# A four-part network on one core: clamps left out, two stage starts reordered, and a batch loop written out

## The chip, the core and the metric

The kernel runs on one core of one Trainium2 chip. The core has a matrix engine (TensorE, PE in the rows, with its weight loads as PEld), VectorE (DVE), ScalarE (ACT), GpSimd (POOL) and SyncE (SP), which in this kernel issues every DMA. Each engine works through its own list of instructions in order and waits on semaphores. The metric is the time of one run on the device in microseconds (us); lower is better.

## The reference, cut to what matters

Batch 8, 512 rows of 256 features, a context of 1024 rows of 192 features, all float32.

```
x = x + xattn0(layernorm(x), ctx)   # 16 heads of 64, softmax over 1024 keys
x = x + experts(layernorm(x))       # router on row 0 picks 2 of 8 experts, gelu MLP 256-256-256, mean
x = x + xattn1(layernorm(x), ctx)   # 16 heads of 16; the keys are the values v
x = x + quantised_mlp(layernorm(x)) # 256-1024-256

# quantised_mlp
W_sim = clip(round(W * s), -128, 127) / s,          s = 127 / max|W| per column or row
x_sim = clip(round(x * t), -32768, 32767) / t,      t = 32767 / max|x|
hidden = gelu(x_sim @ W_in_sim + b_in)
out = quantise_a16(hidden) @ W_out_sim + b_out
```

Since every scale divides by the largest magnitude, the scaled values lie within plus or minus 127 or 32767, up to rounding.

## The kernel before, in words

The four parts run one behind the other, with a barrier of all engines between them. The first attention takes 2006 us of the 3537 us and is not touched.

**Experts** (`experts`). SP loads row 0 of each batch (x8), the first batch's rows, the router's weights, and then the rows of batches 1 to 7 by seven DMAs of 512 KB (line 960). VectorE normalises x8, TensorE computes the router's scores, and VectorE's last routing step (L1083) finds the chosen experts. SP copies the choice to one row by a DMA (line 964), reads an expert's number from it and issues that expert's weights (lines 974 to 980: w1 and w2 of 256 KB, b1, b2), two experts per batch, double-buffered by batch. TensorE (L1016) needs both experts' weights of its batch. VectorE waits for all seven loads before it normalises batch 1.

**Second attention** (`second_attention`). A head prepares batch 0: the projection weights are split in a high and a low float32r part (ScalarE L1579, VectorE L1698), GpSimd fills constant regions (eight memsets, L1727) and then computes the reciprocal deviation (rstd, L1732) for the layer norm; VectorE normalises the rows (L94), TensorE transposes them (L1338) and projects values and queries of head group 0 in three chunks through one PSUM bank, `ps_x` (L1350, L1356), each split by ScalarE (L1539) and VectorE (L1613) before the next may start. Four DMAs spread the queries (qz, L1272), and 32 score blocks are reduced to row maxima (TensorE L1370, VectorE L1619), between which TensorE projects v (L1461). `combine` (L1626) ends the maxima; then the main part starts. It is one body per batch, `batch(b, left)`: four head groups (`attend`: scores, exp on ScalarE L1531, probabilities times v L1397, the next group's maxima), then v of the next batch (L1461) and the output projection with its addition (VectorE L1691). Batches 0 to 5 are one hardware loop per engine (`Fori`), batches 6 and 7 are already written out.

**Last part** (`quantised_layer`). Weights are quantised on VectorE (`quantise_weights`); rows are normalised while they load again; then x is rounded and split, TensorE computes the hidden layer (L2028), ScalarE the gelu (L2043), VectorE each tile's largest value (L1995). The output stage works per batch in four chunks of 1024 columns: VectorE clips and rounds (L2111, L2118), ScalarE subtracts the rounding constant and scales (L2166, L2178), VectorE forms the low part (L2125), TensorE multiplies (L2215, L2217), and VectorE adds the bias and input (`finish`, L2133) for the previous batch behind chunk 1. VectorE rounds three chunks ahead. GpSimd adds the output bias once per batch (L2200). Adding and then subtracting MAGIC (12582912.0) rounds a float32 to an integer.

Of the kernel before, what the change touches and what calls it, by code (L numbers as in the profile page):

```python
# [5 lines left out]
F32 = mybir.dt.float32  # L6
# [882 lines left out]
def experts(nc, x_sb, ident, mhalf, d, x_before):  # L889

    with ExitStack() as ctx:
# [41 lines left out]
        s_x0 = sem("first_x")  # L933
        s_xrest = sem("other_x")
# [18 lines left out]
        def _(sp):  # L953
# [12 lines left out]
            with sp.Fori(0, B // 2) as i:  # L966
                for u in range(2):

                    sp.wait_ge(s_x, QT * (2 * i + u))
                    for k in range(2):  # L970
# [10 lines left out]
                                     ).then_inc(s_w[u], 16)  # L981

# [82 lines left out]
        def _(dve):  # L1065
# [75 lines left out]
def second_attention(nc, x_sb, ident, ident_r, mhalf, d, ctx_parts, x_dram, spare, s_win, s_xs):  # L1141


    with ExitStack() as ctx:
# [55 lines left out]
        s_raw = sem("raw_weights")  # L1200
        s_wh = sem("weights_high")
# [42 lines left out]

        raw_p = prob[:, 0, 0:2, :]
# [11 lines left out]
        def _(sp):  # L1257
            sp.dma_start(raw_p[:, 0], d["v1_wp"][0:P].rearrange("p g n -> p (g n)")).then_inc(s_raw, 16)
            sp.dma_start(raw_p[0:DC1, 1], d["v1_wp"][P:DC].rearrange("p g n -> p (g n)")).then_inc(s_raw, 16)
            sp.dma_start(raw_v[:, 0], d["v1_w"][0:P]).then_inc(s_raw, 16)  # L1260
            sp.dma_start(raw_v[0:DC1, 1], d["v1_w"][P:DC]).then_inc(s_raw, 16)
            sp.dma_start(wqp[:], d["q1_wp"].rearrange("(c k) g n -> k c g n", k=P)).then_inc(s_const, 16)
            for t, a in ((bqp, "q1_b"), (bvp, "v1_bp"), (bv, "v1_b"), (bo, "o1_b")):
                sp.dma_start(t[:], d[a]).then_inc(s_const, 16)
            sp.dma_start(wo[:], d["o1_w"].rearrange("(c p) n -> p c n", p=P)).then_inc(s_const, 16)

# [54 lines left out]
            sp.wait_ge(s_fill, FILLS)  # L1321
# [4 lines left out]
            with sp.Fori(0, B - 2) as b:  # L1326
                batch(b, 2)
# [5 lines left out]
        def _(pe):  # L1333
            def turn_queries(b, c):

                pe.wait_ge(s_ln, 14 * (b + 1))
                for qt in range(QT):
                    mm = pe.transpose(ps_x[:, qt * P:(qt + 1) * P], xn[:, qt, c * P:(c + 1) * P], ident[:])  # L1338
                mm.then_inc(s_tr, 1)

            def project(G, n, c, between=None):


                if c > 0:

                    pe.wait_ge(s_lo, 3 * G + c)
                if c < 2:
                    keys = slice(c * 512, (c + 1) * 512)
                    for step, (context, piece, rows) in enumerate(ctx_weights):
                        mm = pe.matmul(ps_x[:], wvp[0:rows, piece, n, :], context[:, keys],  # L1350
# [4 lines left out]
                else:  # L1355
                    pe.matmul(ps_x[:], wqp[:, 0, n, :], xnT[:, 0, :], start=True, stop=False)  # L1356
                    if between:
                        between(1)
                    pe.matmul(ps_x[:], wqp[:, 1, n, :], xnT[:, 1, :], start=False, stop=True).then_inc(s_kq, 1)
# [140 lines left out]
            pe.wait_ge(s_xnT, DCH)  # L1500
            pe.wait_ge(s_ctx, 48)
            pe.wait_ge(s_const, 16 * NCONST)
# [12 lines left out]

            pe.wait_ge(s_lo, 6)
            max_rows(0, 0)
# [8 lines left out]
        def _(act):  # L1526
# [7 lines left out]
            def split_high(G, n, c):  # L1534
# [789 lines left out]
```

## Time and profile before

| what | value |
|---|---|
| median of 3 runs | 3534.97 us (3531.8 to 3538.29) |
| profiled execution, its own time | 3538.93 us |
| its span | 3537.1 us |
| stretch 0 to 2006.5 us | first attention |
| 2006.5 to 2164.4 us | experts, 157.9 us |
| 2164.4 to 2231.6 us | second attention's head, 67.2 us |
| 2231.6 to 3286.4 us | its eight batches, 1054.8 us |
| 3286.4 to 3340.4 us | last part: weights, normalisation, largest x |
| 3340.4 to 3419.4 us | last part: hidden layer, 79.0 us |
| 3419.4 to 3537.1 us | last part: output stage, 117.7 us |

The span is measured from the first to the last instruction; the execution's own time is 1.8 us longer. Shares of busy time over the whole span hide that each stretch has another engine that is never idle, so the stretches are read one by one.

### The profile page before, as it was taken

What the parts mean: (1) busy time and instruction counts of PE and PEld (TensorE: products, weight loads), DVE (VectorE), ACT (ScalarE), POOL (GpSimd) and SP (SyncE); (2) the same over time, 40 slices, a digit from 0 to 9 for tenths busy, and PEclk for the clock granted to TensorE, in tenths of its full rate; (3) what the DMA queues carried; (4) which work ended last, traced back from release to release, by engine and by line L of the source; (5) the groups of instructions that cost most, each with busy time, mean ns of one, the idle gap of its engine ahead of it and who ended that gap; (6) DMA issues with size and microseconds to landing.
All of it is one profiled execution on the core that took longest, in us unless ns stands there. A gap on an engine that the chain in (4) does not pass through costs nothing. (4 is left out here: it accounts for less than half of the span.)

```text
span 3537.1 us, 49438 instructions
## 1 busy us (share of the span) xinstructions
PE 3266.3 (92%) x14300; PEld 1892.3 (53%) x14300; DVE 2383.8 (67%) x3762; ACT 1675.0 (47%) x1904; POOL 1294.1 (37%) x609
## 2 busy tenths in 40 slices
PE   6999999999999999999999596899999999999576
PEld 4556556555565565565555354455555555554366
DVE  4675675665756756746656243777788778876799
ACT  3443443443434434434434121656556566566376
POOL 1764764756647647746656422000000000000101
PEclk9999999999999999999999897999999999999698
DMA  7564554545544545535355223334334333343202
GB/s 179 118 142 114 119 136 111 129 107 132 131 127 116 132 114 128 138 100 137 98 134 127 81 83 85 86 91 105 88 92 100 93 92 96 97 93 72 67 18 77
DMA packets 265101, 379.07 MB, mean 107 GB/s; under 512 B 35944, under 2 KB 170672, under 8 KB 265008
## 3 DMA queue, kind: packets, MB, share of 16 engines
q1 hardware_dynamic: 265008, 378.06, 43.2%
q8 instruction: 31, 0.51, 0.1%
q14 instruction: 62, 0.51, 0.0%
HBM read 82.22 MB, written 27.26 MB: 31 GB/s over the span
## 5 line engine op out<-in xcount | busy, mean ns | idle before, releaser
L863 POOL TENSOR_TENSOR a_prob_sum<-a_prob_sum,a_prob 128x1024 f32<-128x1024 f32 x384 | 924.2, 2407 | 113.7 <-ACT a_prob L588 88.2
L588 ACT ACTIVATE a_prob<-a_t 128x1024 f32<-128x1024 f32 x512 | 518.2, 1025 | 741.8 <-PE a_t L433 734.5
L1619 DVE TENSOR_REDUCE a_mhalves<-a_m 128x1 f32<-128x512 f32 x1024 | 689.6, 688 | 189.1 <-PE a_m L1370 187.2
L731 DVE TENSOR_REDUCE a_mhalves<-a_m 128x1 f32<-128x512 f32 x1024 | 688.7, 690 | 170.7 <-PE a_m L397 153.0
L1531 ACT ACTIVATE a_prob<-a_t 128x1024 f32<-128x1024 f32 x512 | 498.7, 1023 | 145.5 <-PE a_t L1390 140.6
L1370 PE MATMUL a_m<-a_vh,a_qz 128*128 128x512 f32 x1024 | 463.6, 464 | 36.7 <-DVE a_mhalves L1619 19.9
L440 PE MATMUL a_o<-a_prob,a_v_pair 128*64 128x512 f32 x2048 | 495.4, 605 | 0.0
L397 PE MATMUL a_m<-a_kh_n,a_qz 128*128 128x512 f32 x1024 | 408.1, 429 | 22.0 <-DVE a_mhalves L731 9.8
L863 POOL TENSOR_TENSOR a_prob_sum<-a_prob 128x1024 f32<-128x1024 f32 x64 | 151.6, 2369 | 597.1 <-ACT a_prob L588 597.1
L1370 PEld LDWEIGHTS a_m<-a_vh,a_qz 128*128 128x128 f32 x1024 | 189.9, 189 | 325.1 <-DVE a_mhalves L1619 246.8
L425 PE MATMUL a_t<-a_q_hl,a_k_hh 128*128 128x512 f32 x1024 | 334.6, 408 | 10.5 <-DMA a_k_hh<-a_kh_n 10.1
L1390 PE MATMUL a_t<-a_qs,a_vs 128*128 128x512 f32 x1024 | 323.2, 397 | 3.9 <-ACT a_prob L1531 3.6
L433 PE MATMUL a_t<-a_q_hm,a_k_lm 66*128 66x512 f32 x1024 | 321.7, 395 | 0.0
L397 PEld LDWEIGHTS a_m<-a_kh_n,a_qz 128*128 128x128 f32 x1024 | 182.1, 188 | 238.3 <-DVE a_mhalves L731 103.7
L1732 POOL TENSOR_TENSOR a_rstd<-a_veps,mhalf 128x4 f32<-128x4 f32 x8 | 8.2, 1021 | 820.6 <-DVE a_veps L86 820.4
L1397 PE MATMUL a_o<-a_prob,a_v_all 128*18 128x512 f32 x2048 | 269.7, 598 | 0.4 <-ACT a_prob L1531 0.4
L747 DVE RECIPROCAL a_recip<-a_x 128x128 f32<-128x128 f32 x256 | 232.0, 933 | 51.0 <-PE a_x L455 51.0
L722 DVE TENSOR_TENSOR a_ql_n<-a_x,a_qz 64x512 fp32r<-64x512 f32 x128 | 88.1, 688 | 256.5 <-ACT a_qz L604 254.5
L425 PEld LDWEIGHTS a_t<-a_q_hl,a_k_hh 128*128 128x128 f32 x1024 | 182.8, 188 | 111.4 <-DMA a_q_hl<-a_qz 38.9
L440 PEld LDWEIGHTS a_o<-a_prob,a_v_pair 128*64 128x64 f32 x2048 | 124.3, 136 | 219.6 <-issue 190.6
L1390 PEld LDWEIGHTS a_t<-a_qs,a_vs 128*128 128x128 f32 x1024 | 191.5, 189 | 53.2 <-ACT a_prob L1531 14.4
L433 PEld LDWEIGHTS a_t<-a_q_hm,a_k_lm 66*128 66x128 f32 x1024 | 194.0, 189 | 36.3
(242 smaller groups left out, 4135.0 us busy)
## 6 DMA issues: line engine op xcount, KB each, us to landing
a_k_hh<-a_kh_n SPq DMA_DIRECT2D x256, 256.0 KB, 4.5
a_k_lm<-a_kl_n SPq DMA_DIRECT2D x128, 256.0 KB, 4.9
a_v_pair<-a_v_all SPq DMA_DIRECT2D x64, 512.0 KB, 5.2
a_vs<-a_vh SPq DMA_DIRECT2D x256, 128.0 KB, 2.3
a_wk<-wk_parts SPq DMA_DIRECT2D x64, 256.0 KB, 2.8
a_q_hl<-a_qz SPq DMA_DIRECT2D x128, 128.0 KB, 2.4
a_q_hm<-a_qz SPq DMA_DIRECT2D x128, 128.0 KB, 2.4
a_q_hl<-a_ql_n SPq DMA_DIRECT2D x128, 128.0 KB, 2.4
```

The source lines that it names most:

```text
L397: pe.matmul(ps_m[:, n, :], qz[:, hd, qt * P:(qt + 1) * P], kh_n[:, n * 512:(n + 1) * 512], start=True, stop=True).then_inc(s_mx, 1)
L425: pe.matmul(ps_t[t % 2][:, hd, :], k_hh[:, u, hd, keys], q_hl[:, u, hd, :], start=True, stop=False)
L433: mm = pe.matmul(ps_t[t % 2][:, hd, :], k_lm[0:HD0 + 2, u, hd, keys], q_hm[0:HD0 + 2, u, hd, :], start=False, stop=True)
L440: mm = pe.matmul(ps_o[hd * HD0:(hd + 1) * HD0, :], v_pair[:, pr.set, t, hd * HD0:(hd + 1) * HD0], prob[:, t % RING, hd, :], start=(t == 0) ...
L588: nc.scalar.activation(prob[:, t % RING], ps_t[t % 2][:, :, :], ACT.Exp, scale=SCALE0).then_inc(s_exp, 1)
L731: nc.vector.tensor_reduce(mhalves[:, qt, hd, n:n + 1], ps_m[:, n, :], AX.X, ALU.max).then_inc(s_max, 1)
L863: nc.gpsimd.tensor_tensor(acc, prob[:, (t - 1) % RING] if t == 1 else acc, prob[:, t % RING], ALU.add).then_inc(s_acc, 1)
L1370: pe.matmul(ps_m[:, k, :], qz[:, u, h, qt * P:(qt + 1) * P], vh[:, u, k * 512:(k + 1) * 512], start=True, stop=True).then_inc(s_mx, 1)
L1390: mm = pe.matmul(ps_t[j][:, h, :], vs[:, u, 2 * j + h, keys], qs[:, u, 2 * j + h, :], start=True, stop=True)
L1397: mm = pe.matmul(ps_o[QD * h:QD * h + VW, :], v_all[:, t, GH * n + h, :], prob[:, t % RB, h, :], start=(t == 0), stop=(t == KT - 1))
L1531: nc.scalar.activation(prob[:, t % RB, 2 * j:2 * j + 2, :], ps_t[j][:, :, :], ACT.Exp, scale=SCALE1).then_inc(s_exp, 1)
L1619: nc.vector.tensor_reduce(mhalfs[:, u, qt, h, k:k + 1], ps_m[:, k, :], AX.X, ALU.max).then_inc(s_max, 1)
```

## The change

Five things change.

1. In the last part the clamps are left out: a scaled value is multiplied and MAGIC added in one VectorE instruction, where before one multiplied and took the maximum, and a second took the minimum and added MAGIC. That holds for both weights, for x and for the hidden values.
2. In the experts SP loads batch 1's rows only, then fetches the choice; batch 2's rows go between the weights of batches 0 and 1, the other five batches' rows behind them. VectorE's first three normalisations are written out, each waiting for its own load.
3. In the second attention's head the DMAs, the weight splits, the fills and rstd are reordered by need; the first transposes and projections use three PSUM banks instead of one; v is projected whole ahead of the maxima, and group 1's three projections stand behind maxima 1, 8 and 15.
4. ScalarE fills its eight selector blocks between the splits.
5. Batches 0 to 5 of the second attention are written out on TensorE, ScalarE, VectorE and SP. GpSimd keeps a loop.

SP at the start of the experts, first before (names: `e_w`, `e_b` are the experts' weights and biases, `x_sb` the rows, `e_chosen_row` the choice):

```order
L956 DMA x_sb<-x_first 128x4x256
L957 DMA e_wr<-in_wr 128x2x8
L958 DMA e_br<-in_br 8x8
L960 DMA x_sb<-x_first 128x4x256 x7
L964 DMA e_chosen_row<-e_chosen 1x8x8 [waits e_route_dve]
L966 UNCONDITIONAL_BRANCH [waits e_chosen_row]
L966 ISA
L971 ISA [waits e_x_updated]
L971 TENSOR_LOAD e_chosen_row
L971 ISA x2
L974 ISA
L974 DMA e_w<-in_w 128x2x256
```

Here the fetch of the choice (L964) stands behind all the loads of rows. The same place after:

```order
L958 DMA x_sb<-x_first 128x4x256
L959 DMA e_wr<-in_wr 128x2x8
L960 DMA e_br<-in_br 8x8
L964 DMA x_sb<-x_first 128x4x256
L969 DMA e_chosen_row<-e_chosen 1x8x8 [waits e_route_dve]
L978 TENSOR_LOAD e_chosen_row [waits e_chosen_row]
L978 ISA x2
L981 ISA
L981 DMA e_w<-in_w 128x2x256
L983 DMA e_w<-in_w 128x2x256
L985 ISA
```

The fetch (now L969) stands behind batch 1's rows alone; the rows of batch 2 moved between the weights, the rest behind them.

GpSimd at the start of the second attention, first before (`a_qz` the spread queries, `a_mcol` the maxima's column, `a_qs`, `a_v_all`, `a_wvp`, `a_wv` other constant regions):

```order
L1727 MEMSET a_qs 32x2048
L1727 MEMSET a_qs 32x2048 [waits a1_fills]
L1727 MEMSET a_v_all 128x128x2 [waits a1_fills]
L1727 MEMSET a_v_all 128x128 [waits a1_fills]
L1727 MEMSET a_qz 128x4096 [waits a1_fills]
L1727 MEMSET a_mcol 128x4x96 [waits a1_fills]
L1727 MEMSET a_wvp 64x512 [waits a1_fills]
L1727 MEMSET a_wv 64x256 [waits a1_fills]
L1730 UNCONDITIONAL_BRANCH [waits a1_const,a1_fills]
L1730 ISA
L1732 TENSOR_TENSOR a_rstd<-a_veps,mhalf 128x4 [waits a1_ln_steps]
```

Here rstd (L1732) stands behind all the fills. The same place after:

```order
L1780 MEMSET a_wvp 64x512
L1780 MEMSET a_wv 64x256 [waits a1_fills]
L1772 TENSOR_TENSOR a_rstd<-a_veps,mhalf 128x4 [waits a1_ln_steps,a1_fills]
L1780 MEMSET a_qz 128x4096 [waits a1_rstd]
L1780 MEMSET a_mcol 128x4x96 [waits a1_fills]
L1780 MEMSET a_qs 32x2048 [waits a1_fills] x2
L1780 MEMSET a_v_all 128x128x2 [waits a1_fills]
L1780 MEMSET a_v_all 128x128 [waits a1_fills]
L1787 TENSOR_TENSOR x_sb<-x_sb,a_bo 128x1024 [waits a1_ln_steps,a1_const,a1_fills]
```

rstd stood behind eight memsets and stands behind two; the longest, `a_qz`, now comes directly behind rstd.

VectorE in the output stage, batch 0, first before (`f_hid` hidden values, `f_h_low` their low part):

```order
L2111 TENSOR_SCALAR f_hid<-f_hid,f_amax_h 128x2x512
L2125 SCALAR_TENSOR_TENSOR f_h_low<-f_h_int,f_wout_inv,f_h_high 128x512 [waits f_h_high_ready] x2
L2118 TENSOR_SCALAR f_hid<-f_hid 128x2x512 [waits f_rounding_steps]
L2111 TENSOR_SCALAR f_hid<-f_hid,f_amax_h 128x2x512
L2125 SCALAR_TENSOR_TENSOR f_h_low<-f_h_int,f_wout_inv,f_h_high 128x512 [waits f_h_high_ready] x2
L2118 TENSOR_SCALAR f_hid<-f_hid 128x2x512 [waits f_rounding_steps]
L2111 TENSOR_SCALAR f_hid<-f_hid,f_amax_h 128x2x512
L2125 SCALAR_TENSOR_TENSOR f_h_low<-f_h_int,f_wout_inv,f_h_high 128x512 [waits f_h_high_ready] x2
```

Each chunk has two roundings (L2111, L2118) and the low part (L2125). The same place after:

```order
L2156 TENSOR_SCALAR f_hid<-f_hid,f_amax_h 128x2x512 x4
L2164 SCALAR_TENSOR_TENSOR f_h_low<-f_h_int,f_wout_inv,f_h_high 128x512 [waits f_h_high_ready] x2
L2156 TENSOR_SCALAR f_hid<-f_hid,f_amax_h 128x2x512
L2164 SCALAR_TENSOR_TENSOR f_h_low<-f_h_int,f_wout_inv,f_h_high 128x512 [waits f_h_high_ready] x2
L2156 TENSOR_SCALAR f_hid<-f_hid,f_amax_h 128x2x512
L2164 SCALAR_TENSOR_TENSOR f_h_low<-f_h_int,f_wout_inv,f_h_high 128x512 [waits f_h_high_ready] x2
L2156 TENSOR_SCALAR f_hid<-f_hid,f_amax_h 128x2x512
```

One instruction per chunk (L2118) is gone.

The diff, cut to its core:

```
@@ experts, SP and VectorE
-            for b in range(1, B):
-                sp.dma_start(x_sb[:, b * QT:(b + 1) * QT, :], x_view[:, b * QT:(b + 1) * QT, :]
-                             ).then_inc(s_xrest, 16)
+            load_x(1, 2, s_x1)
             sp.wait_ge(s_rt, 8)
             sp.dma_start(chosen_row[:], chosen[:]).then_inc(s_row, 16)
             sp.wait_ge(s_row, 16)
...
+                    if first and u == 0:
+                        load_x(2, 3, s_x2)
+            load_two(0, True)
+            load_x(3, B, s_xrest)
+            with sp.Fori(1, B // 2) as i:
+                load_two(i, False)
...
-            dve.wait_ge(s_xrest, 16 * (B - 1))
-            with dve.Fori(0, B - 1) as b:
+            for b, landed, count in ((0, s_x1, 1), (1, s_x2, 1), (2, s_xrest, B - 3)):
+                dve.wait_ge(landed, 16 * count)
+                normalise_batch(b + 1)
+                update(b)
+            with dve.Fori(3, B - 1) as b:
@@ second attention, TensorE
+        first_banks = [ps_x[:], ps_m[:, 0, :], ps_m[:, 1, :]]
+        FIRST_PROJECTIONS = (1, 8, 15)
...
             for c in range(DCH):
-                if c:
-                    pe.wait_ge(s_xnT, c)
-                turn_queries(0, c)
...
-            pe.wait_ge(s_wl, 4)
-            pe.wait_ge(s_fill, FILLS)
-            for c in range(3):
-                project(0, 0, c)
+                project(0, 0, c, bank=first_banks[c])
...
             for t in range(KT):
                 project_v(0, t)
-                for c in range(CMB * t // KT, CMB * (t + 1) // KT):
-                    max_scores(0, 0, c)
-                if t in (1, 3, 5):
-                    pe.wait_ge(s_lo, 3 + t // 2)
-                    project(1, 1, t // 2)
+            pe.wait_ge(s_lo, 3)
+            for c in range(CMB):
+                max_scores(0, 0, c)
+                if c in FIRST_PROJECTIONS:
+                    project(1, 1, FIRST_PROJECTIONS.index(c))
...
-            with pe.Fori(0, B - 2) as b:
+            for b in range(B - 2):
                 batch(b, 2)
@@ second attention, ScalarE
-            act.wait_ge(s_raw, 64)
+            act.wait_ge(s_raw, 32)
+            split_weights(tasks[0:2])
             for c in range(DCH):
-                keep_turned(0, c)
+                keep_turned(0, c, first_banks[c])
+            split_high(0, 0, 0, first_banks[0])
+            act.wait_ge(s_rawv, 32)
+            split_weights(tasks[2:4])
...
+            for c in range(3):
+                fill_selectors(0, c)
+                split_high(1, 1, c)
@@ last part
             for t in range(FFT):
-                nc.vector.tensor_scalar(w[:, t, :], w[:, t, :], s[:, t:t + 1], -128.0,
-                                        ALU.mult, ALU.max).then_inc(s_wq, 1)
+                nc.vector.tensor_scalar(w[:, t, :], w[:, t, :], s[:, t:t + 1], MAGIC,
+                                        ALU.mult, ALU.add).then_inc(s_wq, 1)
...
-            nc.vector.tensor_scalar(flat, flat, 127.0, MAGIC, ALU.min, ALU.add).then_inc(s_wq, 1)
...
                     def rounded(b):
-                        nc.vector.tensor_scalar(cols, cols, amax["x"][4][:], -32768.0, ALU.mult, ALU.max
-                        nc.vector.tensor_scalar(cols, cols, 32767.0, MAGIC, ALU.min, ALU.add).then_inc(s_xi, 1)
+                        nc.vector.tensor_scalar(cols, cols, amax["x"][4][:], MAGIC, ALU.mult, ALU.add
...
-                def clipped(b, k):
-                    nc.vector.tensor_scalar(cols, cols, amax["h"][4][:], -32768.0, ALU.mult, ALU.max
-                def rounded(b, k):
-                    nc.vector.tensor_scalar(cols, cols, 32767.0, MAGIC, ALU.min, ALU.add).then_inc(s_r, 1)
+                def rounded(b, k):
+                    nc.vector.tensor_scalar(cols, cols, amax["h"][4][:], MAGIC, ALU.mult, ALU.add
```

## Rows read from the trace of the kernel before

**Rows 1.** Busy time by stretch: us, each engine's busy us (instructions), PEclk, DMA.
```profile
2164.40:2231.60 67.20, 37.40 (x112) 22.45 (x113) 35.71 (x75) 17.13 (x23) 13.96 (x10) 0.70 0.38 102
...
3340.40:3419.40 79.00, 63.76 (x259) 49.33 (x259) 68.72 (x112) 60.33 (x75) 0.00 (x0) 0.93 0.00 0
...
3419.40:3537.10 117.70, 78.38 (x512) 74.02 (x512) 112.83 (x160) 75.96 (x96) 22.00 (x8) 0.82 0.22 72
```

**Rows 2.** Timeline, experts' head: start, us, engine, line, operation [idle before <- releaser].
```profile
2011.64 7.28 SPq L960 DMA_DIRECT2D x_sb<-x_first  x7
...
2015.12 0.15 DVE L1083 FIND_INDEX8 e_chosen<-e_top,e_logits 8x8 uint32<-8x8 f32 x1
...
2027.44 0.40 SPq L974 DMA_DIRECT2D e_w<-in_w  x1
...
2035.13 5.31 PE L1016 MATMUL e_h<-e_xnT,e_w 128*128 x8 [13.39 <-DMA e_b<-in_b]
```

**Rows 3.** Timeline, second attention's head.
```profile
2164.53 3.66 POOL L1727 MEMSET a_qs<- 32x2048 f32 x2 [19.21 <-POOLq L891]
...
2166.90 1.31 DVE L86 TENSOR_SCALAR a_veps<-a_mv 128x4 f32<-128x4 f32 x1
...
2169.05 3.52 POOL L1727 MEMSET a_qz<- 128x4096 f32 x1
...
2174.23 1.03 POOL L1732 TENSOR_TENSOR a_rstd<-a_veps,mhalf 128x4 f32<-128x4 f32 x1 [0.24 <-POOL a_wv L1727]
...
2175.29 1.38 DVE L94 TENSOR_SCALAR spare<-x_sb,a_mv,a_rstd 128x256 f32<-128x256 f32 x4 [7.08 <-POOL a_rstd L1732]
...
2181.20 0.79 PE L1350 MATMUL a_x<-a_ctx_high,a_wvp 128*128 128x512 f32 x1 [1.11 <-ACT spare L1545]
...
2193.29 0.69 ACT L1539 ACTIVATE a_qh<-a_x,a_bqp 128x512 fp32r<-128x512 f32 x1 [4.66 <-PE a_x L1359]
...
2198.12 1.19 PE L1370 MATMUL a_m<-a_vh,a_qz 128*128 128x512 f32 x2 [3.79 <-DMA a_qz<-a_qh]
...
2211.77 2.56 DVE L1619 TENSOR_REDUCE a_mhalves<-a_m 128x1 f32<-128x512 f32 x4
...
2229.78 0.17 DVE L1626 TENSOR_TENSOR a_mcol<-a_mhalves 128x16 fp32r<-128x16 f32 x1
```

**Rows 4.** Windows, v's tiles (L1461) among the maxima: PE and PEld busy, PEclk, DMA.
```profile
2194.40:2229.80 35.40, 6.73 (x35) 6.28 (x35) 0.79 0.42 95
```

**Rows 5.** Timeline, experts, one batch later.
```profile
2056.37 4.18 DVE L94 TENSOR_SCALAR e_xn<-x_sb,e_mv,e_rstd 128x256 f32 x4 [1.13 <-POOL e_rstd L1115]
```

**Rows 6.** Timeline, starts of batches 1, 6 and 7, and where two of them end scores.
```profile
2368.26 0.73 PE L1370 MATMUL a_m<-a_vh,a_qz 128*128 128x512 f32 x2 [1.33 <-DVE x_sb L1691]
...
2369.56 1.28 ACT L1531 ACT_TABLE_LOAD   x1 [6.47 <-PE a_t L1390]
...
2490.99 0.39 PE L1461 MATMUL a_t<-a_wv,a_ctx_high 128*128 128x256 f32 x1
...
3036.63 0.70 PE L1370 MATMUL a_m<-a_vh,a_qz 128*128 128x512 f32 x2 [0.98 <-DVE x_sb L1691]
...
3158.26 0.39 PE L1461 MATMUL a_t<-a_wv,a_ctx_high 128*128 128x256 f32 x1
...
3168.39 0.72 PE L1370 MATMUL a_m<-a_vh,a_qz 128*128 128x512 f32 x2 [0.52 <-DVE x_sb L1691]
```

**Rows 7.** Timeline, last part: VectorE's wait for the rows loaded again.
```profile
3304.05 1.41 DVE L77 BATCH_NORM_STATS2 f_stats<-f_hid 128x6 f32 x4 [2.63 <-DMA f_hid<-x_between]
```

**Rows 8.** Timeline, output stage, two neighbours on VectorE.
```profile
3494.21 0.68 DVE L2118 TENSOR_SCALAR f_hid<-f_hid  x1
...
3494.81 2.88 DVE L2111 TENSOR_SCALAR f_hid<-f_hid,f_amax_h  x1
```

**Rows 9.** Timeline, hidden layer: the one long wait behind the weights' rounding.
```profile
3357.76 1.15 ACT L2037 ACTIVATE f_x_high<-f_xnT,f_minus_magic 128x1024 fp32r x1 [2.44 <-DVE f_xnT L1983]
```

**Rows 10.** Timeline, output stage's start.
```profile
3423.19 5.41 POOL L2200 TENSOR_TENSOR f_xo<-f_xo,f_b_out 128x1024 f32<-128x1024 f32 x2 [92.49 <-DMA f_xo<-x_between]
```

More of the change, by code:

```diff
@@ L958, in _, with load_x @@
             sp.dma_start(br[:], d["br"]).then_inc(s_const, 16)
-            for b in range(1, B):
-                sp.dma_start(x_sb[:, b * QT:(b + 1) * QT, :], x_view[:, b * QT:(b + 1) * QT, :]
-                             ).then_inc(s_xrest, 16)
+            def load_x(first, last, landed):
+                for b in range(first, last):
+                    sp.dma_start(x_sb[:, b * QT:(b + 1) * QT, :], x_view[:, b * QT:(b + 1) * QT, :]
+                                 ).then_inc(landed, 16)
+            load_x(1, 2, s_x1)
             sp.wait_ge(s_rt, 8)
@@ L965, in _, with load_two @@
             sp.wait_ge(s_row, 16)
-            with sp.Fori(0, B // 2) as i:
+            def load_two(i, first):
                 for u in range(2):
-                    sp.wait_ge(s_x, QT * (2 * i + u))
+                    if not first:
+                        sp.wait_ge(s_x, QT * (2 * i + u))
                     for k in range(2):
@@ L1333, in _, with turn_queries, project @@
         def _(pe):
-            def turn_queries(b, c):
+            def turn_queries(b, c, bank=ps_x[:]):
                 pe.wait_ge(s_ln, 14 * (b + 1))
                 for qt in range(QT):
-                    mm = pe.transpose(ps_x[:, qt * P:(qt + 1) * P], xn[:, qt, c * P:(c + 1) * P], ident[:])
+                    mm = pe.transpose(bank[:, qt * P:(qt + 1) * P], xn[:, qt, c * P:(c + 1) * P], ident[:])
                 mm.then_inc(s_tr, 1)
-            def project(G, n, c, between=None):
-                if c > 0:
+            def project(G, n, c, between=None, bank=None):
+                if bank is None and c > 0:
                     pe.wait_ge(s_lo, 3 * G + c)
+                out = ps_x[:] if bank is None else bank
                 if c < 2:
@@ L1349, in project @@
                     for step, (context, piece, rows) in enumerate(ctx_weights):
-                        mm = pe.matmul(ps_x[:], wvp[0:rows, piece, n, :], context[:, keys],
+                        mm = pe.matmul(out, wvp[0:rows, piece, n, :], context[:, keys],
                                        start=(step == 0), stop=(piece == 3))
@@ L1519, in _ @@
             pe.wait_ge(s_oz, 1)
-            with pe.Fori(0, B - 2) as b:
+            for b in range(B - 2):
                 batch(b, 2)
@@ L1532, in exps, with split_high @@
                                      scale=SCALE1).then_inc(s_exp, 1)
-            def split_high(G, n, c):
+            def split_high(G, n, c, bank=ps_x[:]):
                 u = n % 2
@@ L1612, in split_low @@
                 high, low = (vh[:, u, half], vl[:, u, half]) if c < 2 else (qh[:, u, :], ql[:, u, :])
-                nc.vector.scalar_tensor_tensor(low, ps_x[:], (bvp if c < 2 else bqp)[:, n:n + 1], high,
+                nc.vector.scalar_tensor_tensor(low, bank, (bvp if c < 2 else bqp)[:, n:n + 1], high,
                                                ALU.add, ALU.subtract).then_inc(s_lo, 1)
@@ L1710, in _ @@
             normalise_batch(1)
-            with dve.Fori(0, B - 2) as b:
+            for b in range(B - 2):
                 batch(b, 2)
@@ L1729, in _, with add_bias @@
             pool.wait_ge(s_const, 16 * NCONST)
-            with pool.Fori(0, B) as b:
-                pool.wait_ge(s_ln, 14 * b + 10)
-                nc.gpsimd.tensor_tensor(rstd[:], veps[:], mhalf[:, 0:QT], ALU.pow).then_inc(s_rstd, 1)
+            def add_bias(b):
                 pool.wait_ge(s_ln, 14 * b + 14)
@@ L1737, in _ @@
                                         ALU.add).then_inc(s_bias, 1)
-def round_clipped(nc, dve, out, in_, scale, least, most, sem, before):
-    nc.vector.tensor_scalar(out, in_, scale, least, ALU.mult, ALU.max).then_inc(sem, 1)
-    dve.wait_ge(sem, before + 1)
-    nc.vector.tensor_scalar(out, out, most, MAGIC, ALU.min, ALU.add).then_inc(sem, 1)
-    dve.wait_ge(sem, before + 2)
-    nc.vector.tensor_scalar(out, out, MAGIC, None, ALU.subtract).then_inc(sem, 1)
+            add_bias(0)
+            with pool.Fori(1, B) as b:
+                rstd_of(b)
+                add_bias(b)
 def quantised_layer(nc, ident, ones, mhalf, d, x_dram, out, spare, s_win, s_xs):
@@ L2140, in batch @@
                         if after or k < CH - AHEAD:
-                            clipped(*ahead)
+                            rounded(*ahead)
                         low(b, k)
-                        if after or k < CH - AHEAD:
-                            rounded(*ahead)
                         if before and k == 1:
```

128 lines of the change are left out of this document (75 added, 53 removed).

## The prediction

> **What bounds the kernel now.** I read the windows view first, with a cut at each stage, since over the whole span TensorE's 92% hides that the stages have different limits. Three stretches matter [rows 1]. In the head of the second attention (67.20 us) no engine is busy for more than 37.4 us: latency, one thing behind another. In the hidden layer (79.00 us) VectorE has 68.7 us, TensorE 63.8. In the output stage VectorE has 112.83 us of 117.70: it is the bound, at 14.1 us a batch (112.83 / 8), with TensorE at 78.38 (9.8 a batch, granted clock 0.82 on average) and ScalarE at 75.96 (9.5) behind it.
>
> Then the timeline at each place that the change touches. In the experts' head the choice is known at 2015.27, but the first weights are issued at 2027.44, and TensorE, which had ended its work before at 2021.74 (2035.13 less 13.39), starts at 2035.13 on the DMA of the weights [rows 2]. SP's seven row loads stand in between. In the attention's head VectorE waits 7.08 us for rstd, which GpSimd can only compute once its fills are done [rows 3]; the rest is projection, split, DMA and 32 maxima. The batches' starts and score ends give what the loop costs [rows 6].
>
> **The change part by part.** Sums are made on the profiled execution, 3538.93 us; the median of the runs is 3534.97, 3.96 lower, and I take the difference over unchanged.
>
> *Experts, SP's order.* The choice's fetch was issued behind the loads, at 2018.92 at the earliest (2011.64 + 7.28), and first weights followed 8.5 us later. Now it can go at 2015.3, and there is one load's traffic ahead of it instead of seven. If the fetch and reading took those 8.5 us again, weights would be issued at 2023.8: 3.6 us won. But in these 8.5 us the small DMA shares the sixteen engines with 3.5 MB of rows, which the new order leaves for later; I take 3 us for it, so weights at 2018.3. Weights took 7.69 us to TensorE's start (2035.13 - 2027.44) [rows 2], so TensorE starts at 2026.0: 9.1 us won. Ends: 3.6 if the fetch keeps its time; 13.4 if TensorE is no longer kept waiting. Batch 2's rows (512 KB) issued between the weights, and five more batches behind them, could hold batch 1's weights back, but these have a whole batch on TensorE as cover. Value: -9.
>
> *Second attention's head.* rstd stood behind fills until 2174.23. Its input is ready at 2168.2 (2166.90 + 1.31), and that instruction itself took 1.31 us, against 0.17 for L1626, small too, and ended only with GpSimd's fill (2164.53 + 3.66 = 2168.19) [rows 3]. Now two short fills stand ahead, so rstd starts at about 2167.1 and is done at 2168.1, 7.1 us earlier. Directly behind it comes the fill of `a_qz` (3.52 us), beside the four normalisations. Alone these take 1.38 us [rows 3]; in the experts, with GpSimd at work, the same four took 4.18 [rows 5]. So of the 7.1 us some 3 go back; at worst the fills of 3.52 and 1.83 (half of 3.66) stand wholly between them, 5.4; at best nothing. -4.
>
> The first projection to the last query split takes 12.8 us (2181.20 to 2193.98), three turns through one bank, each waiting for the splits of the last. With three banks TensorE needn't wait between them. Ends: 1.4 (two ScalarE splits of 0.69) to 8.5 (two thirds gone). I take -4.5.
>
> Then v. The seven v tiles among the maxima cost TensorE 6.73 us at a granted clock of 0.79 [rows 4], so perhaps 8 ahead of them, where the clock is lower. TensorE waits 3.79 us for the queries' DMA there anyway, and about 1 more now that it is no longer held between projections: 3 us of v sticks out, +3. The maxima, 31.7 us from 2198.12 to 2229.78, lose these interruptions: 32 reductions of 0.64 (2.56 / 4) are 20.5, the first pair 1.2 [rows 3], and for the three projections that remain I leave 4.5: 26.2, so -5.5. ScalarE's selectors leave the path between maxima and exp: -0.4. Head together: -4 - 4.5 + 3 - 5.5 - 0.4 = -11.4, say -11; ends -5 and -20.
>
> The Trainium skill (SBUF — State Buffer, Who interferes with whom) says that GpSimd and VectorE's fast modes share a port pair, whoever issues first holding it for a whole instruction. The 1.31 us that end with the fill agree with it. By it the four normalisations would take turns with the fills of `a_qz` and those behind it, and the sum would take the worst end of that term, 5.4 in place of 3.
>
> *Loop written out.* Batches 1 to 5 ran in the loop, batch 6 written out. Start to start, the loop's took 133.67 us ((3036.63 - 2368.26) / 5), batch 6 131.76 (3168.39 - 3036.63). Of these 1.91 us, 0.81 is the wait at the start (1.33 against 0.52), the hardware loop's turn and its semaphores; 1.10 lies within (122.73 against 121.63 to the end of the scores), where the loop's ScalarE loads its table again each pass, 1.28 us, as TensorE waits [rows 6]. Written out, the order shows one such load. Five starts of 1.91 and the loop's end (0.98 - 0.52): -10. Lower end 5: batch 6 normalises one batch less, which may be part of its lead; upper 12, with batch 0.
>
> *Clamps of weights and x.* The weights' lost instruction shortens VectorE's work, but there VectorE waits 2.63 us for the rows loaded again [rows 7], so it only waits longer: 0. Before the hidden layer x's first clip is on the path, 0.7 to 0.8 us (like the 0.68 of L2118, of the same kind and size [rows 8]), and half of ScalarE's wait of 2.44 us for the next [rows 9] goes, 1.2. Then TensorE holds the stage. -2; ends 0 and -4.
>
> *Output stage.* Each chunk loses an L2118; from its start to the next instruction's is 0.60 us (3494.81 - 3494.21) [rows 8]. 8 batches of 4 are 32 x 0.60 = 19.2. At the start GpSimd's two additions (5.41 us) [rows 10] hold up VectorE in any case: a multiplication beside one of these additions took 2.88 us [rows 8], where one alone takes about what its neighbour does, 0.68. I take off 2.2, one such stretch. At the end ScalarE's steps follow each other, 1 off. -16. A batch then takes 14.1 - 2.4 = 11.7 us, still over TensorE's 9.8 and ScalarE's 9.5. Ends: -19 and -9, the latter if another engine's chain shows through, 1.2 us a batch.
>
> Sum: -9 - 11 - 10 - 0 - 2 - 16 = -48; 3534.97 - 48 = 3487.
>
> **The rivals.** *The output stage meets another bound* (-38): its granted clock is 0.82 on average, so part of it runs at 1.2 GHz [rows 1]. Wholly at that level TensorE's 9.8 us a batch would be 16 (9.8 x 0.82 x 2), over the new 11.7. For it: the clock is already low at 67% of busy time (78.38 / 117.7). Against: in a shorter stage the same work stands denser. It would take back 10 of the 16.
>
> *The loop costs nothing* (-38): batch 6 is quicker only because it lacks work, or written-out code starts worse. For: it is one batch. Against: a table load and a start wait which both are seen to differ.
>
> *The head gains little* (-42): fills hold the normalisations for the whole 5.4 us, and v stands ahead at the lower clock, so that its head gains 5. For: the instruction that ended with the fill [rows 3]. Against: the experts' four normalisations lost 2.8 beside GpSimd (4.18 - 1.38), not 5.4 [rows 3, 5].
>
> *All goes better* (-59): no hold by the fills, v covered by the queries' DMAs, weights sooner. Speaks for it that TensorE, denser in the head, could get its higher clock sooner; against it, rows 5 again.
>
> *Slower than before* (+8 or more): the written-out code. On four engines the second attention's program grows from three bodies to eight and an engine that has to wait for its instructions holds all. Its place would be the start of each batch. The other terms bring -38, so it decides from 6.3 us more in each of batches 0 to 5 (38 / 6), and 7.7 make it +8. Against it, batch 6, written out and run once, starts with a wait of 0.98 and batch 7 with 0.52, where the loop had 1.33 [rows 6].
>
> **How the numbers follow.** Chances: forecast 0.60, output stage bound 0.12, loop nothing 0.09, head little 0.08, all better 0.08, slower 0.03. A measurement can't tell less than 0.2% (7 us) from no change. The five cases that gain lie far beyond it: 0.97. The slower case's 0.03 splits into 0.02 slower and 0.01 within. The range: the terms' ends, added as independent ones, are some 14 us either way of 3487, and the rivals that gain less stand at 3493 to 3497, the better one at 3476. So 3472 to 3500, which leaves out the slower case and the far ends of the others.
>
> **What would show it.** SP issues the first weights at about 2018, TensorE's first expert product comes at 2026. Four normalisations take 1.4 to 4.2 us and not the 6.8 that 1.38 + 5.4 would make. `combine` comes 11 us earlier counted from the stage's start. Batches 0 to 5 take some 131.8 us, with one table load. L2118 has no successor, and the additions of the output (`finish`) come 11.7 us apart a batch. Wrong would be: weights issued at 2023 or later (fetch's time not due to traffic); v's tiles ending after a queue of idle maxima of more than 3 us; batches at 133.7; an output stage where VectorE waits for TensorE or ScalarE.

## The result, and the profile after

The changed kernel takes 3477.85 us (median of 4 runs, 3476.89 to 3480.76) against 3536.63 us for the one before in the same comparison (4 runs, 3531.80 to 3539.99): ratio 0.9836, 95% interval 0.9819 to 0.9853, 58.8 us less. The forecast was 48 less, 3487 us with a range of 3472 to 3500. The profiled executions differ by 61.2 us (3538.93 and 3477.76), and the trace, cut at the stages' first instructions, says where:

| stretch | before, us | after, us | change | forecast |
|---|---|---|---|---|
| first attention (same code) | 2006.48 | 2004.92 | -1.6 | 0 |
| experts | 158.04 | 149.21 | -8.8 | -9 |
| second attention, start to `combine` | 65.26 | 54.10 | -11.2 | -11 |
| `combine` to the last rows' store | 1056.65 | 1047.29 | -9.4 | -10 |
| last part: weights, normalisation | 54.03 | 54.07 | 0.0 | 0 |
| last part: hidden layer | 78.92 | 77.08 | -1.8 | -2 |
| last part: output stage | 117.72 | 89.23 | -28.5 | -16 |

Five terms came out within 1 us; the output stage gave 12.5 us more than its term. The windows view of the kernel after (length; busy us and count of PE, PEld, DVE, ACT, POOL; granted clock; DMA), for the attention's head, the hidden layer and the output stage, answers to [rows 1]:

```profile
2154.13:2208.23 54.10, 36.31 (x108) 21.34 (x108) 39.90 (x65) 16.79 (x22) 12.56 (x10) 0.72 0.52 139
...
3309.59:3386.67 77.08, 63.26 (x259) 49.43 (x259) 63.98 (x102) 61.03 (x75) 0.00 (x0) 0.94 0.00 0
...
3386.67:3475.90 89.23, 70.89 (x512) 68.43 (x512) 84.22 (x128) 73.44 (x96) 26.02 (x8) 0.86 0.28 95
```

VectorE is still the busiest engine of the output stage (84.22 of 89.23), TensorE's clock rose from 0.82 to 0.86, and GpSimd's eight additions cost it 26.02 us in place of 22.00.

The timeline of the experts' head, against [rows 2]:

```profile
2013.53 0.15 DVE L1097 FIND_INDEX8 e_chosen<-e_top,e_logits 8x8 uint32<-8x8 f32 x1
...
2016.51 0.40 SPq L981 DMA_DIRECT2D e_w<-in_w  x1
...
2024.82 5.48 PE L1030 MATMUL e_h<-e_xnT,e_w 128*128 x6 [4.68 <-DMA e_b<-in_b]
```

The first weights are issued 2.8 us after the choice (2016.51 against 2013.68), and TensorE starts 8.3 us later. From the stage's first instruction TensorE's start moved from 28.65 to 19.90 us.

The timeline of the attention's head, against [rows 3]; the stage starts at 2154.13:

```profile
2156.35 1.02 POOL L1772 TENSOR_TENSOR a_rstd<-a_veps,mhalf 128x4 f32<-128x4 f32 x1 [1.33 <-DVE a_veps L86]
...
2157.41 7.97 DVE L94 TENSOR_SCALAR spare<-x_sb,a_mv,a_rstd 128x256 f32<-128x256 f32 x4 [1.21 <-POOL a_rstd L1772]
...
2157.44 3.52 POOL L1780 MEMSET a_qz<- 128x4096 f32 x1
...
2161.51 3.72 POOL L1780 MEMSET a_qs<- 32x2048 f32 x2
...
2167.76 0.77 PE L1371 MATMUL a_x<-a_ctx_high,a_wvp 128*128 128x512 f32 x1 [0.35 <-ACT spare L1571]
...
2173.52 0.69 ACT L1565 ACTIVATE a_qh<-a_m,a_bqp 128x512 fp32r<-128x512 f32 x1 [0.77 <-PE a_m L1380]
...
2178.44 0.63 PE L1391 MATMUL a_m<-a_vh,a_qz 128*128 128x512 f32 x2
...
2208.23 0.18 DVE L1664 TENSOR_TENSOR a_mcol<-a_mhalves 128x16 fp32r<-128x16 f32 x1
```

rstd comes 7.5 us earlier in the stage, but the four normalisations, 1.38 us before, take 7.97: from rstd to 2165.38, which is 0.15 us after the second of the fills at 2161.51 ends. One by one they took 3.68, 0.58, 1.97 and 1.97 us, beside fills of 3.52, 0.44 and two of 1.86. So the normalised rows are only 0.9 us earlier in the stage. The three projections then follow each other: 6.5 us from the first (2167.76) to the last split's end (2174.21), where there were 12.8. The maxima start 4.2 us after that, as before (4.1), and take 29.8 us (31.7).

The starts of batches 1, 6 and 7, against [rows 6]:

```profile
2346.11 0.73 PE L1391 MATMUL a_m<-a_vh,a_qz 128*128 128x512 f32 x2 [0.65 <-DVE x_sb L1729]
...
3005.86 0.74 PE L1391 MATMUL a_m<-a_vh,a_qz 128*128 128x512 f32 x2 [0.65 <-DVE x_sb L1729]
...
3137.69 0.73 PE L1391 MATMUL a_m<-a_vh,a_qz 128*128 128x512 f32 x2 [0.52 <-DVE x_sb L1729]
```

Batches 1 to 5 take 131.95 us each ((3005.86 - 2346.11) / 5), batch 6 takes 131.83.

In the output stage, one place where VectorE and GpSimd meet, against [rows 8]:

```profile
3444.34 1.40 DVE L2164 SCALAR_TENSOR_TENSOR f_h_low<-f_h_int,f_wout_inv,f_h_high 128x512 fp32r<-128x512 f32 x2
...
3444.40 3.61 POOL L2236 TENSOR_TENSOR f_xo<-f_xo,f_b_out 128x1024 f32<-128x1024 f32 x1 [6.51 <-DMA f_xo<-x_between]
...
3445.66 1.65 DVE L2172 SCALAR_TENSOR_TENSOR f_xo<-f_y,f_amax_h,f_xo 128x256 f32<-128x256 f32 x4
...
3447.23 1.34 DVE L2156 TENSOR_SCALAR f_hid<-f_hid,f_amax_h  x1
```

and GpSimd's addition in the kernel before that goes with the multiplication of 2.88 us there:

```profile
3494.39 2.76 POOL L2200 TENSOR_TENSOR f_xo<-f_xo,f_b_out 128x1024 f32<-128x1024 f32 x1 [11.31 <-DMA f_xo<-x_between]
```

In what follows the hold is the time by which an instruction of VectorE takes longer beside GpSimd than it does alone, and the period is the time from one batch's `finish` to the next. In both kernels GpSimd's addition starts about 7.2 us after the end of a `finish`: the finished rows are stored, the next ones loaded, then it adds. With batches of 14.06 us it started at 3494.39, while VectorE had a multiplication next (3494.81), which then ended only at 3497.69. With batches of 10.1 us it starts beside `low` (L2164) and `finish` (L2172), which keep their 1.40 and 1.65 us; here it is the addition that gets longer, 3.61 us for 2.76, and only the end of it holds the multiplication at 3447.23, 1.34 us in place of 0.74. The hold per batch fell from 2.14 to 0.60 us.

Each of the eight additions holds one instruction of VectorE. In the kernel before these are six multiplications of 2.84 to 2.88 us and, at the start and at the end, one instruction of a `low` pair each, 2.82 and 2.86 us in place of 0.70. In the kernel after the two additions at the start cost as much as before, and the other six about 0.6 us each.

### The profile page after: what moved, and what is told of

It reads as the page before. It is cut to its first block and busy times, and to the rows that moved or that the text cites. A ratio compares the mean times of both kernels' runs of the same rounds, so it can differ in the third digit from the quotient of the medians.

```text
span 3475.9 us, 46403 instructions
## 1 busy us (share of the span) xinstructions
PE 3260.8 (94%) x14300; PEld 1888.5 (54%) x14300; DVE 2353.9 (68%) x3720; ACT 1666.7 (48%) x1899; POOL 1296.5 (37%) x609
```

## The experiments

Times are medians; the untouched first attention ends anywhere from 2000.9 to 2009.9 us in these profiles, so effects of a few us are read from the stage's own length. How well a stage repeats in profiles where it was not edited: the experts take 157.6 to 158.3 us in the kernel before, E1 to E4 and E13, and 148.3 to 149.6 in the kernel after, E5 to E7, E11 and E12; the second attention's head takes 63.5 to 66.3 us in the kernel before and E1 to E4, and 51.8 to 54.1 in the kernel after, E6 to E9 and E11. So terms of the head under 2 us are read from single traces and are no more than that. E1 to E4 and E13 start from the kernel before, the others from the kernel after.

**E1, no addition of the output bias, kernel before.**

```
-nc.gpsimd.tensor_tensor(xo[:, u], xo[:, u], bout..., ALU.add).then_inc(s_b, 1)
+pool.sem_inc(s_b, 1)
```

> The kernel before, with GpSimd's addition of the output bias left out of the output stage (so the bias is missing from the output); nothing else changed. Theory H (the addition holds VectorE's multiplication, 2.88 us in place of 0.74, once a batch): the period of the output stage falls from 14.06 to about 11.9 us, the stage by 17 us with the two additions at its start, the run by 0.5%. Rival W (the hold only shifts idle time, VectorE would wait for TensorE or ScalarE instead): period 13.5 or more, the run less than 0.15% faster.

**E2, only the output stage's rounding changed, kernel before.** Its output section is that of the kernel after:

```
-    clipped(*ahead)          # multiply, max
+    rounded(*ahead)          # multiply, add MAGIC
     low(b, k)
-    rounded(*ahead)          # min, add MAGIC
```

> The kernel before with only the output stage's two roundings made one; its limits, weights, x, head and loop unchanged. Theory H (where GpSimd's addition falls among VectorE's instructions changes with the period, and the hold shrinks from 2.1 to 0.6 us a batch): the stage falls from 117.7 to about 89 us, period 10.1, the run 28 us (0.8%) faster. Rival C (the extra 12 us of the output stage come from the other changes, as the clock or the hidden layer's end): the stage falls only by the 16 to 17 us of the removed instructions, period 11.7.

**E3, both.**

> As the run before it, and GpSimd's addition of the output bias left out too (the bias is missing from the output). Theory H: the period is VectorE's own work, 4 x (0.66 + 1.33) + 1.57 = 9.5 us, or ScalarE's 9.1 if that shows; the stage is 82 to 84 us, so 5 to 7 us below the run with the addition, against 17 us that leaving it out gives with two roundings. Rival C: the same difference with and without the second rounding.

Measured: E1 3516.34 us, ratio to before 0.9946 (0.9929 to 0.9962); E2 3509.81, 0.9926 (0.9910 to 0.9943); E3 3501.51, 0.9904 (0.9888 to 0.9921). E1 and E3 leave the output bias out of the result. The output stage's windows, one row from each kernel's trace, E1, E2, E3:

```profile
3415.75:3515.90 100.15, 72.76 (x512) 68.48 (x512) 95.88 (x160) 75.78 (x96) 0.00 (x0) 0.90 0.25 84
```

```profile
3422.65:3512.20 89.55, 71.74 (x512) 69.61 (x512) 84.21 (x128) 73.44 (x96) 25.97 (x8) 0.85 0.28 94
```

```profile
3418.08:3501.00 82.92, 65.95 (x512) 63.31 (x512) 76.90 (x128) 73.00 (x96) 0.00 (x0) 0.95 0.31 102
```

| output stage, us (period) | with the additions | without | difference |
|---|---|---|---|
| two roundings | 117.72 (14.06) | 100.15 (11.92) | 17.6 |
| one rounding | 89.55 (10.1) | 82.92 (9.52) | 6.6 |
| difference | 28.2 | 17.2 | |

Theory H holds, its rivals W and C fall: the run of E1 is 18.5 us faster, E2 alone reproduces the stage of the kernel after (89.23), and without the additions the removed instruction is worth 17.2 us, what its own duration says (32 x 0.60 = 19.2, less 1 to 2). The other 11 us come with the additions: what they cost fell from 17.6 to 6.6 us. The trace shows how, a hold of 0.6 in place of 2.1 us in each batch but at the start.

**E4, the addition in four pieces, kernel before.**

```
-tensor_tensor(xo[:, u], xo[:, u], bout (all 4 row tiles))
+for qt in range(QT): tensor_tensor(xo[:, u, qt], xo[:, u, qt], bout[:]).then_inc(s_b, 1)
```

> The kernel before with GpSimd's addition of the output bias in four pieces of 256 columns, each signalled by itself, where it was one of 1024. If VectorE's multiplication is held for as long as one GpSimd instruction that was there first runs, it now waits for a piece (about 0.7 us) and the hold falls from 2.1 to some 0.3 to 0.7 us a batch: stage 10 to 12 us shorter. Rival: it waits until GpSimd has no work left, and nothing changes (stage 117 to 118 us).

Measured: 3534.15 us, ratio 1.0003 (0.9993 to 1.0012); stage 114.46 us, period 13.9. The rival (no change, 117 to 118 us) is nearer, but both expectations missed what happens. Timeline:

```profile
3490.79 4.46 POOL L2201 TENSOR_TENSOR f_xo<-f_xo,f_b_out 128x256 f32<-128x256 f32 x4 [9.44 <-DMA f_xo<-x_between]
...
3491.16 1.23 DVE L2111 TENSOR_SCALAR f_hid<-f_hid,f_amax_h  x1
...
3492.31 2.35 DVE L2125 SCALAR_TENSOR_TENSOR f_h_low<-f_h_int,f_wout_inv,f_h_high 128x512 fp32r<-128x512 f32 x2
...
3494.59 1.22 DVE L2118 TENSOR_SCALAR f_hid<-f_hid  x1
```

The multiplication (L2111) is held for 0.5 us only, but then `low` takes 2.35 us in place of 1.40 and L2118 1.22 in place of 0.68: more instructions of VectorE are held, each for a shorter time, and VectorE loses 2.0 us a batch, nearly as before (2.14). The addition itself takes 4.46 us in place of 2.76.

**E5, the fills behind the normalisations, kernel after.**

```
     rstd_of(0)
-    pool.wait_ge(s_rstd, 1)
+    pool.wait_ge(s_ln, 14)
```

> The kernel after, with GpSimd's six remaining fills held back until VectorE's four normalisations of batch 0 are done. Theory P (the fills hold the normalisations, 7.97 us in place of 1.38): they take 1.4 us, the first transposes come 6.6 us earlier, and `combine` 3 to 6 us earlier, less where the context, the weights' split or the fill before the queries' DMA is late next; the run 0.1 to 0.17% faster than the kernel after. Rival D (the normalisations are slow because of the DMAs' traffic into the same memory): they still take 5 us or more and nothing moves.

Measured: 3470.64 us (3470.52 to 3474.48), ratio to before 0.9817 (0.9804 to 0.9829), 7.2 below the kernel after; only part of this is the edit, since the first attention and the experts, where nothing changed, are 3.0 us shorter in this profile. Timeline; the stage starts at 2151.17:

```profile
2154.45 1.38 DVE L94 TENSOR_SCALAR spare<-x_sb,a_mv,a_rstd 128x256 f32<-128x256 f32 x4 [1.21 <-POOL a_rstd L1772]
...
2155.89 3.52 POOL L1780 MEMSET a_qz<- 128x4096 f32 x1 [1.48 <-DVE spare L94]
...
2160.39 0.80 PE L1371 MATMUL a_x<-a_ctx_high,a_wvp 128*128 128x512 f32 x1 [2.54 <-DMA a_ctx_tail<-ctx_parts]
```

The normalisations take 1.38 us again, which is theory P. Now the first projection waits 2.54 us for the context's DMA, which takes part of the gain: `combine` is 49.87 us into the stage, 4.2 earlier than in the kernel after, and 1.9 to 3.4 earlier than in E6 to E9 and E11, which have the same head.

**E6, all four engines in a loop again; E7, ScalarE alone; E11, VectorE alone.** Kernel after, for each engine named:

```
-for b in range(B - 2):
+with dve.Fori(0, B - 2) as b:
     batch(b, 2)
```

> The kernel after, with batches 0 to 5 of the second attention in one hardware loop per engine again, on TensorE, ScalarE, VectorE and SyncE. Theory: batches 1 to 5 take 133.7 us again in place of 131.95, 9 us in all over the stage, 0.25% slower than the kernel after. Rival: the shorter batches come from the new head and not from the loop, and they stay at 132.

> The kernel after, with the loop on ScalarE alone; TensorE, VectorE and SyncE keep their written-out batches. Theory T (the activation table loaded again in each pass, 1.28 us while TensorE waits for the exponentials, makes the 1.1 us inside a batch): batches of about 133.1 us, +6 us in all. Rival L (the turn of the loops of TensorE and VectorE makes it): 132.0 to 132.3 us, less than +2 us.

> The kernel after, with batches 0 to 5 in a loop on VectorE alone. With all four looped VectorE's first reduction of a batch came 2.95 us after its last instruction with nothing that the profile shows to wait for, and TensorE waited 1.8 us for it with a clock that then fell. Theory B (that is VectorE's branch back, with instructions that are not there yet): batches of 134.5 to 135.5 us, +16 to +20 us in all. Rival S (it comes from several loops together, or the place of SyncE's): 132 to 132.5.

Measured: E6 3500.78 us, ratio to before 0.9898 (0.9884 to 0.9913); E7 3481.70, 0.9844 (0.9832 to 0.9857); E11 3496.96, 0.9889 (0.9874 to 0.9905). Batches 1 to 4 take 136.5 us in E6, 133.0 in E7, 136.6 in E11, where the kernel after has 131.95 and the one before 133.7. E7 is theory T: ScalarE's loop, with its table load, is 1.07 us a batch. E6 missed both expectations: the loop costs 4.6 us a batch here. E11 finds it: VectorE's loop alone costs as much, more than the 134.5 to 135.5 us that its theory B expected. The costs do not add up: E6 has the table load and a wait of 1.33 us at each batch's start besides (E7 0.66, E11 0.65), and its batches are no longer than E11's. Why is open. Timeline of E11 at the start of a batch:

```profile
2614.43 0.73 PE L1391 MATMUL a_m<-a_vh,a_qz 128*128 128x512 f32 x2 [0.66 <-DVE x_sb L1729]
...
2617.36 1.29 DVE L1657 TENSOR_REDUCE a_mhalves<-a_m 128x1 f32<-128x512 f32 x2 [2.98 <-issue]
...
2618.10 0.80 PE L1391 MATMUL a_m<-a_vh,a_qz 128*128 128x512 f32 x1 [2.47 <-DVE a_mhalves L1657]
```

VectorE's first reduction comes 2.98 us after its last instruction, with nothing that the profile shows to wait for ("issue"); its operand was there at about 2615. TensorE waits 2.47 us for the bank. In the ten us from a batch's start the granted clock is then lower, 0.66 in E11 and E6, 1.00 in the kernel after. TensorE's busy time, granted clock and DMA, E6 first, then the kernel after:

```profile
2485.61:2495.61 10.00, 8.19 (x26) 0.66 0.57 147
```

```profile
2478.06:2488.06 10.00, 9.82 (x46) 1.00 0.70 177
```

**E13, the loop moved in VectorE's program, kernel before.**

```
-nc.vector.memset(ps_o[:], 0.0)
+for n in range(54): nc.vector.memset(ps_o[:, 8 * n:8 * n + 8], 0.0)
+nc.vector.memset(ps_o[:, 432:512], 0.0)
...
-pe.wait_ge(s_oz, 1)
+pe.wait_ge(s_oz, 55)
```

> The kernel before, in which VectorE's one fill at the start of the second attention is written as 55 smaller ones, so that its loop over the batches stands 54 instructions later in its program, as it does in the kernels with VectorE's loop and the new head; the loop itself and all other engines' programs are the same. Theory A (what a turn of VectorE's loop costs depends on where the loop lies in the program): batches of 136 to 137 us in place of 133.7, and the run 14 to 18 us slower, of which 3 us are the fills. Rival B (it depends on what the other engines do, which are written out or otherwise ordered there): 133.7, and the run 3 us slower.

Measured: 3552.79 us, ratio 1.0040 (1.0026 to 1.0054), 14.5 us slower; batches 135.7 to 136.6 us. Timeline of E13, and behind it the first reduction of a batch in the kernel before:

```profile
2637.75 0.72 PE L1370 MATMUL a_m<-a_vh,a_qz 128*128 128x512 f32 x2 [1.33 <-DVE x_sb L1691]
...
2640.00 1.29 DVE L1619 TENSOR_REDUCE a_mhalves<-a_m 128x1 f32<-128x512 f32 x2 [2.98 <-issue]
...
2640.74 0.79 PE L1370 MATMUL a_m<-a_vh,a_qz 128*128 128x512 f32 x1 [1.81 <-DVE a_mhalves L1619]
```

```profile
2502.47 3.27 DVE L1619 TENSOR_REDUCE a_mhalves<-a_m 128x1 f32<-128x512 f32 x5 [1.26 <-PE a_m L1370]
```

Theory A: the loop's body and the other engines' programs are the same, but for the number that TensorE waits for once ahead of the loop, and the 2.98 us of "issue" are there, where the kernel before waited 1.26 us, for TensorE. What a turn of the loop costs depends on where it lies in the program. The granted clock of a batch's first ten us goes with it: 1.00 in the kernel before (133.7 us a batch), 0.83 in E13's batches 1 and 2 (135.7 and 135.9), 0.66 in its batches 3 and 4 (136.5 and 136.6). The Trainium skill (Runtime: NRT & Kernel Launch, Instruction fetch mechanics) says that a taken branch whose target is outside the pages held forces a fetch before execution goes on. The longer stop at the loop's first instruction fits that, but no run here shows a fetch, so the cause of the 2.98 us is not shown.

**E8, all rows ahead of the choice; E9, the choice's fetch early, then all rows, then weights.** Kernel after:

```
 load_x(1, 2, s_x1)
+load_x(2, 3, s_x2); load_x(3, B, s_xrest)      # E8
 sp.wait_ge(s_rt, 8)
 sp.dma_start(chosen_row[:], chosen[:]).then_inc(s_row, 16)
+load_x(2, 3, s_x2); load_x(3, B, s_xrest)      # E9
...
-load_x(2, 3, s_x2)          # both, among and behind the first weights
-load_x(3, B, s_xrest)
```

> The kernel after, with all seven loads of rows issued ahead of the fetch of the choice again. Theory: the first weights are issued 19 to 21 us after the stage's start in place of 11.6, TensorE's first expert product comes 8 to 9 us later, and the whole run by as much, 0.25%. Rival: VectorE's written-out waits gave part of the gain, and it loses only 3 to 5 us.

> The kernel after, with the fetch of the choice issued at its new, early place, but the rows of batches 2 to 7 issued directly behind it and ahead of the first weights. Theory T (the fetch was slow in the kernel before, 8.5 us, since rows were on their way): the fetch is done while SyncE still issues rows, weights are issued when it is through, about 18 us after the stage's start, and then wait for 3 MB of rows, so TensorE starts at 26 to 27 us in place of 19.9: 6 to 7 us lost. Rival O (only the fetch's own time matters): TensorE starts within 2 us of where it did.

Measured: E8 3482.01 us, ratio to before 0.9849 (0.9836 to 0.9861); E9 3482.66, 0.9854 (0.9839 to 0.9869). TensorE's first expert product comes 27.88 us after the stage's start in E8 and 26.07 in E9, against 19.90; the stages last 156.63 and 154.62 us against 149.21. E8's stage gives back 7.4 us and E9's 5.4, a little under the expected 8 to 9 and 6 to 7; the runs' medians lie only 4.2 and 4.8 us above that of the kernel after. In E8 the fetch is issued at 2015.30, behind seven loads, and the first weights follow 8.3 us later (2023.59), where the changed order takes 2.8. SyncE and TensorE in E9:

```profile
2012.75 0.78 SPq L969 DMA_DIRECT2D e_chosen_row<-e_chosen  x1
...
2013.58 4.27 SPq L964 DMA_DIRECT2D x_sb<-x_first  x6
...
2018.90 0.39 SPq L983 DMA_DIRECT2D e_w<-in_w  x1
...
2029.97 5.31 PE L1029 MATMUL e_h<-e_xnT,e_w 128*128 x8 [10.79 <-DMA e_b<-in_b]
```

Weights went out 1.1 us after the last of the rows, so the fetch had been under way while these were issued; yet TensorE started only 11.1 us after the weights' issue, where it was 8.3. Theory T holds: TensorE starts at 26.07 us, in its 26 to 27, though the weights are issued 3 us sooner than it said (15.0 us after the stage's start, not 18).

**E12, the fills behind, and the bias of batches 0 to 6 added in the second attention.** GpSimd adds it to each batch's rows there once they are stored, SyncE stores them a second time (`x_res`), and the output stage loads these; one addition is left.

```
+def add_out_bias(b):                     # GpSimd, second attention
+    pool.wait_ge(s_xs, 16 * (b + 1))
...
+    nc.gpsimd.tensor_tensor(xb, xb, bo2..., ALU.add).then_inc(s_xr, 1)
...
-dve.wait_ge(s_b, b + 1)                  # finish
+dve.wait_ge(s_xl[u], 16 * (i + 1))
```

> The kernel after with the fills behind the normalisations, and with the output bias of batches 0 to 6 added by GpSimd in the second attention, to rows that are stored a second time for the output stage, instead of in the output stage. If GpSimd's additions are what holds VectorE there, the output stage falls from 89.2 to 83 or 84 us (one addition is left), and with combine 4 us earlier the run is at about 3464 to 3466 us. Rival: GpSimd's 2.4 us a batch in the attention, and 3.6 MB more of stores and loads, cost there what is won, and it stays at 3470.

Measured: 3465.74 us (3463.54 to 3466.80), ratio to before 0.9803 (0.9789 to 0.9816): the fastest, 12.1 us below the kernel after. Its output stage:

```profile
3380.12:3463.60 83.48, 66.84 (x512) 64.39 (x512) 77.48 (x128) 73.00 (x96) 2.64 (x1) 0.93 0.31 101
```

83.48 us, and the batches keep their 131.9 to 132.0 us: with TensorE busy for 1021.30 of the main part's 1047.29 us in the kernel after, the additions there cost next to nothing.

## Why the prediction was right, and where it was off

The direction and five of six terms were right; the sum fell 11 us short of the medians' difference (58.8), and one term accounts for it.

- *Output stage, -16, measured -28.5.* The step that failed: "At the start GpSimd's two additions (5.41 us) [rows 10] hold up VectorE in any case", from which 2.2 us were taken off, one such stretch. The 2.88 us of [rows 8] were read as a feature of the start, where they stand in every batch. VectorE's 112.83 us held eight such stretches, and subtracting 0.60 a chunk took the hold as fixed work, although it depends on what VectorE has next when GpSimd begins. E1 to E3 split it: 17.2 us for the instructions, near the 16 forecast, and 11.0 for a smaller hold, which the prediction had at nothing. A batch takes 10.1 us, not 11.7.
- *Experts, -9, measured -8.8.* Right in its two parts: the fetch took 2.8 us (3 taken), and the weights 8.3 (7.7). E8 shows the fetch suffer from rows ahead of it (8.3 us), E9 the weights (11.1).
- *Attention's head, -11, measured -11.2,* but by errors that cancel. Normalisations: -4 forecast, -0.9 measured, since they took 7.97 us, beyond even the end of 6.8 that I had called the worst. E5 shows that the fills do it: there were four of them beside the normalisations (3.52, 0.44, 3.72 for two), where the prediction counted two. The Trainium skill (SBUF — State Buffer, Who interferes with whom) has the engine that issues first hold the shared port pair for a whole instruction; the trace agrees, with one normalisation to each fill. Banks: -4.5 forecast, -6.3 measured, and 2.1 more between the normalised rows and the first projection, where the transposes use two of the banks. v: +3 forecast, 0 measured; the granted clock was 1.00 from 2172.50 to 2178.44, while v ran. Maxima: -5.5 forecast, -1.9 measured: the clock fell after the first few, and a pair of maxima took 1.58 us in place of 1.28. In the kernel before it was the other way round, 1.00 for the last 20.2 us of the maxima (2209.60 to 2229.78). No run changes the banks, v or the maxima alone, so these parts are read from the two traces and not tested. TensorE's busy time, clock and DMA in the maxima of the kernel after, in two pieces:

```profile
2178.44:2184.30 5.86, 4.38 (x15) 1.00 0.72 160
...
2184.30:2208.23 23.93, 19.36 (x33) 0.65 0.55 124
```

- *Loop, -10, measured -9.4.* The two parts came out: 1.07 us of table load a batch (1.10; E7), and 0.68 at the start of each (0.81). The second was not tested alone: the start's wait is 0.66 us with the loop on ScalarE, 0.65 with it on VectorE and 1.33 with all four, which points to the loops of TensorE or SyncE. That nothing more came was luck: the kernel before stood at a place where VectorE's loop turned without the 2.98 us of "issue". At the place of E13 its batches take 3.8 to 4.6 us more than written out, in place of 1.8.
- *Weights and x, 0 and -2, measured 0.0 and -1.8.* Read from the stages' lengths; no run changes them alone.
- *The rivals.* TensorE never became the bound of the output stage (-38 did not come; its clock rose). The slower outcome had the sign of the effect wrong: not the written-out code but, in E11 and E13, the loop's turn costs time at a batch's start. "All goes better" (-59) names nearly the measured time, by luck: of its reasons v's cover came true, the absence of a hold by the fills did not, and the output stage, which made the difference, is not in it.

## What to carry to other kernels

Subtract from an engine's busy time only what an instruction costs alone: where one is much longer than its like, find out what holds it and whether the edit moves the two apart. Put GpSimd's work where VectorE waits for others anyway (E12), or beside instructions that keep their time, as `finish` did, which reads one of its inputs from PSUM; cutting it in pieces hardly helped (E4). Before believing in the price of a hardware loop, look at the first instruction behind its branch: its price can change with an edit somewhere else in the program.

## What the runs showed of the hardware that I had not expected

- VectorE's normalisations took turns with GpSimd's fills, one for one: 7.97 us for four of them in place of 1.38 (E5), with the fills at their usual length.
- A VectorE loop turned without a stop of its own in one place and with 2.98 us of "issue" in another, 54 instructions later (E13); with TensorE's lower clock behind it this made 2.0 to 2.9 us a batch there, and 4.6 in the kernel after (E11).
- Removing work also moved an overlap: one instruction of 0.60 us per chunk, taken out, saved 2.4 us a batch by itself, and another 1.5 because GpSimd's addition then fell beside other instructions.
